# Softmax codes written by GpSimd as 16-bit integers and multiplied as they are, without VectorE's copy

## The reference, cut to what matters

```
def _fq(x, delta, zp, n_bits):
    xi = _round_ste(x / delta) + zp
    xq = jnp.clip(xi, 0.0, 2.0 ** n_bits - 1.0)
    return (xq - zp) * delta
...
sim = jnp.einsum('bhid,bhjd->bhij', _fq(q, dq, 128.0, 8), _fq(k, dk, 128.0, 8)) * SCALE
attn = jax.nn.softmax(sim, axis=-1)
out = jnp.einsum('bhij,bhjd->bhid', _fq(attn, dw, 0.0, 8), _fq(v, dv, 128.0, 8))
```

## Time and profile before

| what | value |
|---|---|
| median of three runs | 1584.53 us |
| the profiled execution, its own time | 1576.92 us |
| its span in the profile | 1575.1 us |
| busy over the span: PE / DVE / ACT / POOL | 69% / 70% / 57% / 43% |
| quantised self stage, first to last code instruction on POOL | about 691 to 1001 us |
| quantised cross stage | about 1001 to 1163 us |
| VectorE's copies (L2047), 192 of them | 103.1 us busy |
| GpSimd's code instructions (L2289), 512 of them | 299.7 us busy |

### The profile page before, as it was taken

The page is one execution under the profiler, slowest core; times in us unless marked ns, Lnnn a source line. Parts: engine busy times, 40 slices in busy tenths (PEclk is TensorE's granted clock), DMA queues, the critical chain, the costliest instruction groups (busy, mean ns, idle before and its releaser), DMA issues.

```text
span 1575.1 us, 28607 instructions
## 1 busy us (share of the span) xinstructions
PE 1092.8 (69%) x9344; PEld 593.3 (38%) x9344; DVE 1098.1 (70%) x3102; ACT 894.2 (57%) x2546; POOL 681.1 (43%) x1055
## 2 busy tenths in 40 slices
PE   2888888887788797855353545444358778888888
PEld 1333344444333286831120212222225435453545
DVE  2687777777688653678888999877765666666522
ACT  1555554555554464567676797988852344646531
POOL 3321011011011416558888888877741344445310
PEclk9899999999999998975555555555569799999989
DMA  5213142101331112267555576665530121201000
GB/s 184 61 53 92 51 129 75 54 24 50 99 106 49 42 39 82 57 160 122 99 104 109 106 130 115 121 109 106 109 57 14 27 48 35 49 21 43 1 0 27
DMA packets 265219, 116.53 MB, mean 74 GB/s; under 512 B 216936, under 2 KB 253936, under 8 KB 262896
## 3 DMA queue, kind: packets, MB, share of 16 engines
q1 hardware_dynamic: 260112, 108.29, 30.8%
q0 software_dynamic: 2048, 4.20, 0.9%
q10 hardware_dynamic: 2912, 2.22, 0.5%
HBM read 38.80 MB, written 16.45 MB: 35 GB/s over the span
## 4 chain that ended last, share of the span: by engine, by line
PE 35%; POOL 21%; DVE 18%; issue 14%; ACT 9%; DMA 1%; SPq 0%; POOLq 0%; another core or an unknown queue 0%; ACTq 0%; DVEq 0%
POOL arena L2289 12%; ACT arena L1581 4%; PE acc L1199 3%; POOL inv_total L2278 2%; PE trans L1171 2%; DVE minus_top L1980 2%; PE misc L1021 2%; PE misc L1027 2%; PE trans L1323 2%; ACT arena L1528 2%; PE score L1335 2%; PE score L1337 2%; PE trans L1177 1%; POOL arena L2235 1%; PE acc L1385 1%
## 5 line engine op out<-in xcount | busy, mean ns | idle before, releaser
L2289 POOL TENSOR_SCALAR arena<-arena,inv_total 128x512 f16<-128x512 f32 (+1 forms) x512 | 299.7, 585 | 57.3 <-DVE inv_total L2058 16.8
L1980 DVE TENSOR_REDUCE minus_top<-score 128x4 f32<-128x616 f32 (+4 forms) x256 | 200.6, 802 | 95.3 <-PE score L1141 36.9
L2154 POOL TENSOR_TENSOR rstd<-spread,minus_half 128x4 f32<-128x4 f32 x36 | 37.5, 1043 | 489.5 <-DVE spread L1662 414.0
L1581 ACT ACTIVATE arena<-score,minus_top,exp_scale 128x512 f32<-128x512 f32 (+1 forms) x340 | 210.4, 625 | 20.9 <-POOL arena L2289 11.9
L1528 ACT ACTIVATE arena<-trans 128x512 f32<-128x512 f32 x240 | 134.4, 596 | 109.3 <-PE trans L1177 104.0
L1619 ACT ACTIVATE arena<-arena,minus_top 128x154 f32<-128x154 f32 x256 | 105.2, 412 | 129.3 <-DVE minus_top L2123 129.1
L1280 PE MATMUL score<-arena 32*128 32x512 bf16 (+1 forms) x340 | 68.9, 458 | 139.7 <-ACT arena L1581 138.7
L2064 DVE TENSOR_REDUCE top_score<-score 128x2 f32<-128x1024 f32 (+1 forms) x128 | 135.7, 1061 | 0.6 <-PE score L1280 0.5
L2309 POOL TENSOR_TENSOR arena<-arena,inv_total 128x512 f32<-128x512 f32 x64 | 66.5, 1040 | 143.9 <-DVE inv_total L2131 130.0
L1581 ACT ACTIVATE arena<-trans,minus_top,exp_scale 128x154 f32<-128x154 f32 (+1 forms) x172 | 105.5, 620 | 19.2 <-POOL arena L2289 14.9
L2118 DVE CUSTOM_DVE_ANT_0 arena<-score,arena 128x154 f32<-128x154 f32 x256 | 65.9, 313 | 60.6 <-PE score L1360 60.2
(11 more groups left out here) (283 smaller groups left out, 2814.4 us busy)
## 6 DMA issues: line engine op xcount, KB each, us to landing
arena<-q_terms SPq DMA_DIRECT2D x88, 128.0 KB, 2.8
late<-arena SPq DMA_DIRECT2D x128, 64.0 KB, 2.0
q_terms<-arena SPq DMA_DIRECT2D x36, 128.0 KB
late<-k_terms SPq DMA_DIRECT2D x32, 128.0 KB, 3.1
arena<-arena SPq DMA_TRANSPOSE x192, 3.1
by_expert<-zeros SPq DMA_DIRECT2D x2, 1472.0 KB, 9.8
arena<-by_expert SPq DMA_DIRECT2D x10, 256.0 KB
from_expert<-arena SPq DMA_DIRECT2D x10, 256.0 KB
```

The costliest lines, as they stand in the source:

```text
L1581: ins = nc.scalar.activation(probs[:, i % 3, j, of], quant_score[i % 3][:, j, of], ACT.Exp, bias=minus_top[:, at_col:at_col + 1], scale=ex ...
L1980: nc.vector.tensor_reduce(dst, src, axis=AX.X, op=ALU.max, negate=True).then_inc(top_ready, 1)
L2289: ins = nc.gpsimd.tensor_scalar(codes[:, (i - 1) % CODE_SOURCES, j, to], probs[:, (i - 1) % 3, j, of], inv_total[:, at_col:at_col + 1], HA ...
```

## The change

`copy_codes` goes, with its semaphore `codes_copied` and its lag of six steps. GpSimd's instruction keeps its multiplication, but its second operation is now a minimum with 255 in place of the addition of 1024, and it writes through a view of the same `codes` bytes as 16-bit unsigned integers. The write rounds. The transposed bytes are read by TensorE as fp16: the integer n is there the number n times 2^-24. The output scale takes up the factor 2^24, once, in the setup. The value codes become fp16, since both operands of a product have one type. The transpose writes straight into `pT_codes`. `weigh_pair` waits for the two transposes themselves. Nothing else moves, and `WEIGH_LAG` stays at eight.

```
-HALF_ROUND = 1024.0
+CODE_STEP = 2.0 ** -24
-QUANT_LAG, WEIGH_LAG, GROUPED_LAG = 6, 8, 2
+WEIGH_LAG, GROUPED_LAG = 8, 2
...
-        v_quant, v_quant_tail = put([P, 2, TILES, HEADS, 32], bf16), put([P, 2, HEADS, 32], bf16)
+        v_quant, v_quant_tail = put([P, 2, TILES, HEADS, 32], fp16), put([P, 2, HEADS, 32], fp16)
...
-        pT_codes = put([P, CODE_SLOTS, 2 * TILES, P], bf16)
-        put = place(arena, [pT_at])
-        pT_raised = put([P, CODE_SLOTS, 2 * TILES, P], fp16)
+        pT_codes = put([P, CODE_SLOTS, 2 * TILES, P], fp16)
...
         codes = put([P, CODE_SOURCES, 2, TOKENS], fp16)
+        code_numbers = codes.rearrange("p i j k -> p (i j k)").bitcast(mybir.dt.uint16)
+        code_numbers = code_numbers.rearrange("p (i j k) -> p i j k", i=CODE_SOURCES, j=2)
...
-                    nc.vector.tensor_scalar(out_scale[:, n:n + 1], vv, w, None, ALU.mult)
+                    nc.vector.tensor_scalar(out_scale[:, n:n + 1], vv, w, 1.0 / CODE_STEP, ALU.mult, ALU.mult)
...
-                    sp.dma_start_transpose(pT_raised[:, i % CODE_SLOTS, :, :],
+                    sp.dma_start_transpose(pT_codes[:, i % CODE_SLOTS, :, :],
...
-                    pe.wait_ge(codes_copied, 2 * n + 2)
+                    for i in (2 * n, 2 * n + 1):
+                        pe.wait_ge(codes_turned[i % CODE_SLOTS], 16 * (i // CODE_SLOTS + 1))
...
-                    nc.vector.tensor_scalar(pT_codes[:, of, :, :].rearrange("p k q -> p (k q)"),
-                                            pT_raised[:, of, :, :].rearrange("p k q -> p (k q)"),
-                                            -HALF_ROUND, 255.0, ALU.add, ALU.min).then_inc(codes_copied, 1)
...
-                                ins = nc.gpsimd.tensor_scalar(codes[:, (i - 1) % CODE_SOURCES, j, to], probs[:, (i - 1) % 3, j, of],
-                                                              inv_total[:, at_col:at_col + 1], HALF_ROUND, ALU.mult, ALU.add)
+                                ins = nc.gpsimd.tensor_scalar(code_numbers[:, (i - 1) % CODE_SOURCES, j, to], probs[:, (i - 1) % 3, j, of],
+                                                              inv_total[:, at_col:at_col + 1], 255.0, ALU.mult, ALU.min)
```

More of the change, by code:

```diff
@@ L555, in build @@
         qT_codes, k4_codes = put([P, 2, TOKENS], bf16), put([P, 2, 4, TOKENS], bf16)
-        v_quant, v_quant_tail = put([P, 2, TILES, HEADS, 32], bf16), put([P, 2, HEADS, 32], bf16)
+        v_quant, v_quant_tail = put([P, 2, TILES, HEADS, 32], fp16), put([P, 2, HEADS, 32], fp16)
         probs = put([P, 3, 2, TOKENS])
-        pT_at = quant_at[0]
-        pT_codes = put([P, CODE_SLOTS, 2 * TILES, P], bf16)
-        put = place(arena, [pT_at])
-        pT_raised = put([P, CODE_SLOTS, 2 * TILES, P], fp16)
+        pT_codes = put([P, CODE_SLOTS, 2 * TILES, P], fp16)
         put = place(arena, [0])
         codes = put([P, CODE_SOURCES, 2, TOKENS], fp16)
+        code_numbers = codes.rearrange("p i j k -> p (i j k)").bitcast(mybir.dt.uint16)
+        code_numbers = code_numbers.rearrange("p (i j k) -> p i j k", i=CODE_SOURCES, j=2)
         put = place(arena, quant_at)
@@ L675, in build @@
         codes_ready = sem("codes_ready")
-        codes_copied = sem("codes_copied")
         pair_weighed = sem("pair_weighed")
@@ L1343, in feed_forward @@
                     downs(B - 1)
-                pe.wait_ge(codes_copied, len(QUANT_STEPS))
                 pe.wait_ge(quant_exp, len(QUANT_STEPS))
@@ L2041, in of_step @@
                     return z if heads > 1 else z.rearrange("p j i -> p (j i)")
-                def copy_codes(i):
-                    of = i % CODE_SLOTS
-                    dve.wait_ge(codes_turned[of], 16 * (i // CODE_SLOTS + 1))
-                    nc.vector.tensor_scalar(pT_codes[:, of, :, :].rearrange("p k q -> p (k q)"),
-                                            pT_raised[:, of, :, :].rearrange("p k q -> p (k q)"),
-                                            -HALF_ROUND, 255.0, ALU.add, ALU.min).then_inc(codes_copied, 1)
                 quant_steps = len(QUANT_STEPS)
@@ L2065, in _ @@
                                                 negate=True).then_inc(quant_top, 1)
-                    if QUANT_LAG <= i < quant_steps + QUANT_LAG:
-                        copy_codes(i - QUANT_LAG)
                     if i in QUANT_LAST:
```

## The result

The changed kernel takes 1923.94 us (median of four runs, 1920.65 to 1932.52), against 1582.53 us for the kernel before, measured beside it. The ratio is 1.216, with a 95% interval of 1.210 to 1.223. The forecast was 1557 us, so it had the sign wrong, and the time lies far outside the range of 1543 to 1580 and beyond the 1690 us of rival 1 too.

A forecast was written before the change was run, and what follows sets the result against it. GpSimd was taken to lead the self stage's first half, DVE and ACT the second, ACT the cross stage. Gains of 20 (self), 7 (cross) and 0.4 us (end), 27.4 in all, took 1584.5 to 1557 us, range 1543 to 1580.

The forecast's parts named there:

- rival 1: GpSimd's code instruction: the minimum or integer write makes it dearer, kernel slower, about 1690 us at the upper end; chance 0.14.
- (g): GpSimd's code instruction: minimum for addition and integers for fp16 change its time by 0; upper end 1040 ns.
- (a): VectorE: 192 copies leave, 74.1 us in the self stage and about 28 us elsewhere, no gain by itself.
- (b): GpSimd in the self stage: stretching by the copies goes, 13.5 us, about half of it in each half.
- (c): Self stage: room on DVE removes most of ACT's waits for maxima; whole stage gains 20 us, bounds 13.5 and 24.8.
- rival 3: Self stage: only GpSimd's stretching by the copies comes off, 13.5 us, about 1571 us; counted inside the forecast's 0.77.
- (d): Cross stage: ACT leads, its waits for DVE's maxima shrink around unit changes, 7 us gained, bounds 0 and 11.7.
- (e): TensorE's wait for the transposes in `weigh_pair`: they land long before, no cost; 0.4 us gained at the end.
- (f): Transposes: issue at 1.23 us and landing of 3.1 us fit the faster pace, DMA share about 0.75, no cost.
- (h): TensorE's types: 16-bit products before and after, no cost; the setup's extra multiplication is nothing.

The follow-up runs named there:

- the first experiments: Kernel before with only the minimum put in, copies and fp16 kept: 1922 us; changed kernel with an addition of 0 for the minimum: 1543 us.
- the working version: Changed kernel with an addition of 0 for the minimum, bound left out (ratio 0.977) or held on the factor (ratio 0.981).
- the timed run: Changed kernel with an addition of 0 in place of the minimum, bound left out: 1546.5 us against 1582.7, ratio 0.977.
- the last version: Changed kernel with an addition of 0 for the minimum and the bound at 255 held on the factor: 1550.2 us against 1583.0, ratio 0.981.

## Why the prediction was wrong

**The step that failed is (g).** It took 0 for the new form of GpSimd's instruction, with an upper end of 1040 ns from the dearest near row. It costs 2005 ns, and the first experiments put the whole of it on the minimum. "Same shape, same bytes, same two operations: the nearest row is L2289 itself" was the error: the row shows the same engine and shape but another operation, and on this engine that turned out to be no near row. The slope of 0.82 ns per element was read as the cost of moving elements, which it may well be for that form. It bounds nothing for another form. Measured between 154 and 512 elements, the slopes are:

| second operation | 128x512 / 128x154, ns | ns per element | from |
|---|---|---|---|
| addition of 0 | 699 / 401 | 0.83 | the integer write alone |
| multiplication by 1 | 699 / 399 | 0.84 | two multiplications |
| none | 1569 / 683 | 2.47 | a multiplication alone |
| minimum with 255 | 2005 / 822 | 3.30 | the changed kernel |
| maximum with 0 | 2002 / 810 | 3.33 | the maximum |

**Rival 1 was right in its mechanism and in its place, and too small.** It named L2279, the minimum, and the point from which it decides (0.06 us; it was 1.3 us). With the measured price in its own working, a self step is 1.93 + 2 x 1.31 = 4.55 us, where the timeline has 4.35 to 4.45, and 128 steps of 4.35 us are 310 us over the clean pace. Its time of 1690 us rested on an upper end that was the price of another operation. The rule of the Trainium skill that stood beside it (GPSIMD Engine Reference, section 7) would have made a minimum cost 1.03 to 2.03 cycles per element; measured are 3.30 ns, about 4 cycles at the 1.2 GHz which the same page states (section 1). It pointed the right way and was too low by half. The rule cited for no change (section 3.1, up to two operations bound by the port at 1.03 cycles, 0.86 ns) agrees with the two arithmetic pairs alone (0.83 and 0.84 ns); a single multiplication costs 2.47 ns per element. A chance of 0.14 for an instruction that no row showed, on the engine that led, was too low.

**Steps (a), (b), right in kind and a little too large.** The copies' stretching of POOL came off for the most part, 721 to 703 ns and 338 to 297 ns in the run with the copies alone removed. Put into the sum of (b), these are 254 x 18 + 127 x 41 ns = 9.8 us, where 13.5 were taken.

**Step (c), too large.** The self stage gained 10 us from the copies' removal, not 20, which is under the lower bound of 13.5 and about what the stretching measured. Room on DVE did not remove most of ACT's waits for maxima (38.0 to 32.5 us, not to under half). In the unit change shown, the late maximum stands behind DVE's own wait for PE and the norm; that the others do too is not shown. What I had set apart as rival 3, (b) alone, at 1571, is nearly what the copies are worth: 18 us, interval 11 to 23.

**Step (d).** The cross stage went from 161.6 to 1145.0 - 988.2 = 156.8 us in the same run (from the last scaling of the self stage to the last code instruction): 5 us, where 7 were taken, inside its bounds.

**Steps (e), (f), (h).** No cost to speak of from the transposes at the pace of the working version (in the timed run GpSimd waited for one once, 2.2 us), and products at 306 to 307 ns in fp16 as in bf16. PE did wait 6.7 us in two places for a transpose in the cross stage of the timed run, up to 4.1 us each, which (e) said would never be. It is no new cost, though: in the kernel before, PE waited 9.0 us in three places of that stage for the copy. The row of the timed run:

```profile
PE acc L1299 <- DMA arena<-arena: 6.7, 2, 4.1
```

**The sum of 27 us comes near the gain of the working versions (30 to 44 us in the timed run, 31 us by the ratio 0.981 of the last version) by luck.** The copies' removal is worth 18 of it. About 10 more come with the addition of 0 in place of 1024, by the shorter pair, which no step had.

## What to carry to other kernels

An operation that the trace does not show on an engine is not priced by an instruction of the same shape with another operation. On GpSimd, measure the form first. A single multiplication on a wide tile was quicker written as an arithmetic pair (multiply and add 0, or multiply by 1). A bound can go on the narrow factor where the wide values are themselves bounded, as exponentials of a softmax are. When a copy is taken off an engine that works in order, look at what stands in front of the late instruction there; free time on that engine doesn't shorten its waits for others.

## What the runs showed of the hardware

- GpSimd's `tensor_scalar` from fp32 to 16 bits takes 0.83 ns per element for multiply-add and 0.84 for multiply-multiply, 2.47 for a multiplication alone, and 3.3 for multiply-minimum and multiply-maximum. The minimum costs this whether it writes fp16 (2013 ns for 128x512) or 16-bit integers (2005 ns).
- Writing 16-bit unsigned integers costs what writing fp16 costs (699 and 700 ns, both with 0 added).
- GpSimd writes fp16 numbers as small as 2^-24 at that price too, and TensorE multiplies such numbers in 306 ns, as bf16 before (307 ns).
- Two such instructions in a row take 1.46 us where 1024 is added, and 1.36 to 1.37 us with an addition of 0 or a multiplication by 1. The cause stays open.
